# Linear attention on Trainium2: the turned query tile's affine steps and the key sums move from ScalarE to VectorE

## What is computed

```python
    qh = _split_heads(_layernorm(q @ wq, ln_gamma, ln_beta))
    kh = _split_heads(_layernorm(k @ wk, ln_gamma, ln_beta))
    vh = _split_heads(_layernorm(v @ wv, ln_gamma, ln_beta))
    q_prime = jax.nn.relu(qh) + EPS_K
    k_prime = (jax.nn.relu(kh) + EPS_K) * em
    vh = vh * em
    kv = jnp.einsum('bhnd,bhne->bhde', k_prime, vh)
    z = 1.0 / (jnp.einsum('bhnd,bhd->bhn', q_prime, k_prime.sum(axis=-2)) + EPS_K)
    att = jnp.einsum('bhnd,bhde,bhn->bhne', q_prime, kv, z)
```

## Time and profile before

| | us |
|---|---|
| median of three runs | 740.03 |
| the three runs | 743.93, 737.79, 740.03 |
| the profiled execution | 745.89 |
| its span in the profile | 744.1 |
| first stage in it | from the start to about 165 |

### The profile page before, as it was taken

One profiled execution on the slowest core, in us unless ns is written; L12 is line 12 of the kernel. 1 busy time (PEld: TensorE's weight loads), 2 busy tenths in 40 slices (PEclk: granted clock), 3 DMA queues, 4 the chain that ended last, 5 costly groups with the idle time before them and its releaser, 6 DMA issues.

```text
span 744.1 us, 19421 instructions
## 1 busy us (share of the span) xinstructions
PE 666.2 (90%) x7317; PEld 467.4 (63%) x7317; DVE 522.7 (70%) x1228; ACT 519.2 (70%) x875; POOL 270.2 (36%) x324
## 2 busy tenths in 40 slices
PE   6888889885468999999999999999999987999997
PEld 5677778773225666666665566566666664577777
DVE  5898889978778779878878878878876751212112
ACT  6788889878326887887787787787888866634441
POOL 6788889882243214304322422432233100000000
PEclk9999999999589999999999999999999999799999
DMA  5122222525523476356547636645664480201110
GB/s 186 43 84 83 83 83 83 160 86 31 121 74 86 92 167 142 92 130 135 128 92 142 152 92 145 135 109 111 135 155 114 87 192 8 61 30 57 29 43 26
DMA packets 59523, 74.42 MB, mean 100 GB/s; under 512 B 35464, under 2 KB 40322, under 8 KB 59450
## 3 DMA queue, kind: packets, MB, share of 16 engines
q1 hardware_dynamic: 59450, 73.39, 41.8%
HBM read 32.35 MB, written 1.40 MB: 45 GB/s over the span
## 4 chain that ended last, share of the span: by engine, by line
PE 42%; issue 12%; DVE 10%; POOL 5%; ACT 2%; SPq 1%; DMA 1%; DVEq 0%; POOLq 0%; ACTq 0%
PE ps L832 7%; PE ps L844 7%; PE ps L771 7%; PE ps L683 6%; DVE mx L1694 6%; PE ps L758 5%; PE ps L669 3%; PE ps L675 3%; POOL Qb L1221 2%; POOL QD L1235 1%; ACT P L1096 1%; DVE kvall L1525 1%; POOL KP L1207 1%; PE ps L705 1%; SPq L450 1%
## 5 line engine op out<-in xcount | busy, mean ns | idle before, releaser
L1096 ACT ACTIVATE P<-ps,kbias,kscale 125x896 f32<-125x896 f32 x192 | 210.3, 1097 | 86.2 <-PE ps L758 83.4
L1694 DVE TENSOR_REDUCE mx<-ps 128x1 f32<-128x500 f32 x336 | 213.9, 671 | 46.4 <-PE ps L683 45.0
L683 PE MATMUL ps<-KP,Qb 128*128 128x500 bf16 x336 | 128.8, 385 | 15.1 <-DVE mx L1694 9.9
L1207 POOL TENSOR_TENSOR KP<-kvall,KP 128x1500 bf16<-128x1500 f32 x16 | 48.6, 3038 | 230.8 <-ACT KP L1039 230.8
L771 PE MATMUL ps<-P,Vp 125*32 125x112 f32 x3072 | 113.6, 265 | 2.7 <-ACT P L1096 1.4
L771 PEld LDWEIGHTS ps<-P,Vp 125*32 125x32 f32 x3072 | 67.4, 109 | 53.0 <-issue 37.8
L543 PE MATMUL ps<-wkv,cT 128*125 128x256 f32 x384 | 93.0, 386 | 4.9 <-ACT wkv L895 4.9
L543 PEld LDWEIGHTS ps<-wkv,cT 128*125 128x125 f32 x384 | 69.8, 191 | 13.7 <-ACT wkv L895 4.9
L1157 ACT ACTIVATE arena<-ps,b 128x448 f32<-128x448 f32 x64 | 40.4, 633 | 47.5 <-PE ps L832 41.6
L561 PE MATMUL ps<-arena 125*128 125x130 f32 x384 | 54.9, 285 | 17.5 <-DVE arena L1399 15.1
L758 PE MATMUL ps<-QS,KS 128*128 128x112 bf16 x768 | 68.7, 214 | 1.4 <-DVE QS L1700 1.4
(11 more groups left out here) (217 smaller groups left out, 1031.1 us busy)
## 6 DMA issues: line engine op xcount, KB each, us to landing
cT<-ctxT_dram SPq DMA_DIRECT2D x31, 750.0 KB, 4.1
KS<-KP SPq DMA_DIRECT2D x48, 375.0 KB, 7.3
arena<-KP SPq DMA_DIRECT2D x48, 375.0 KB, 7.2
QS<-QD SPq DMA_DIRECT2D x96, 28.0 KB, 5.5
wgu<-w_dram SPq DMA_DIRECT2D x8, 256.0 KB, 3.2
silu<-w_dram SPq DMA_DIRECT2D x8, 256.0 KB, 3.0
x<-xh_dram SPq DMA_DIRECT2D x1, 512.0 KB, 4.0
cT<-ctxT_dram SPq DMA_DIRECT2D x1, 500.0 KB, 5.3
```

The costliest lines, as they stand in the source:

```text
L683: ins = nc.tensor.matmul(ps[:, bank, 0:KCW], q[:, 128 * c:128 * c + 128], KP[par][0][:, KCW * k:KCW * k + KCW], start=True, stop=True)
L1096: nc.scalar.activation(P[t % 2][0:TK, :].rearrange("p (k n) -> p k n", k=2), src, ACT.Exp, scale=kscale[0:TK, bass.ds(n, 1)], bias=kbias[0 ...
L1207: nc.gpsimd.tensor_tensor(KP[par][2][:], krest, KP[par][1][:], ALU.subtract).then_inc(sem("kp3_ready"), 1)
L1694: ins = v.tensor_reduce(mx[:, c, k:k + 1], ps[:, bank, 0:KCW], AX.X, ALU.max)
```

## The change

The relu and affine step of the turned query tile and its added constant, two ScalarE instructions, become two VectorE instructions: scale and shift by the two columns of `affine`, from PSUM to the same place in PSUM, and then maximum with 0 and the added constant, from PSUM to SBUF. Between them VectorE waits for its own result. They stand in the step of group 1, behind the keys, for tiles 0 to 6; for the last tile they stand in the end stage between the last state but one and the last clamp. The copy of the key sums goes from ScalarE to VectorE too, ahead of the state it belongs to; the wait of VectorE for ScalarE's copy goes. TensorE waits for the finished query tile where it waited for the relu.

```diff
                     if par == 0:
-                        pe.wait_ge(sem("qT_relu"), b // 2)
+                        pe.wait_ge(sem("qT_ready"), b // 2)
...
-            def turned_query(i, bank):
-
-                nc.scalar.activation(qT[:, bass.ds(D * i, D)], ps[:, bank, 0:D], ACT.Relu, scale=affine[:, 0:1],
-                                     bias=affine[:, 1:2]).then_inc(sem("qT_relu"), 1)
-
-            def raised_query(i):
-
-                cols = bass.ds(D * i, D)
-                nc.scalar.activation(qT[:, cols], qT[:, cols], ACT.Identity, bias=eps_in[:]).then_inc(sem("qT_ready"), 1)
...
-            def key_sums(b, par):
-
-                act.wait_ge(sem("kv_done"), NG * (b + 1) + SLOTS)
-                nc.scalar.copy(ks2[:, par:par + 1], ps[:, 6 + par, D:D + 1]).then_inc(sem("ks2_ready"), 1)
...
+            def turned_query(i, bank):
+
+                dve.wait_ge(sem("qT_ps"), i + 1)
+                v.tensor_scalar(ps[:, bank, 0:D], ps[:, bank, 0:D], affine[:, 0:1], affine[:, 1:2], ALU.mult,
+                                ALU.add).then_inc(sem("qT_normed"), 1)
+                dve.wait_ge(sem("qT_normed"), i + 1)
+                v.tensor_scalar(qT[:, bass.ds(D * i, D)], ps[:, bank, 0:D], 0.0, EPS_IN, ALU.max,
+                                ALU.add).then_inc(sem("qT_ready"), 1)
...
             def state(b, par):
 
                 dve.wait_ge(sem("kv_done"), NG * (b + 1) + SLOTS)
-                dve.wait_ge(sem("ks2_ready"), b + 1)
                 kv = ps[:, 6 + par, :]
+                v.tensor_copy(ks2[:, par:par + 1], kv[:, D:D + 1]).then_inc(sem("ks2_ready"), 1)
...
+                        if k == 1 and not first:
+                            turned_query(i - 1, 6)
...
             state(B - 2, 0)
+            turned_query(NT - 1, 3)
             relu(last, SLOTS - 1)
```

More of the change, by code:

```diff
@@ L975, in pair @@
                             query_rows(k - 3, 7)
-                        if g == 0 and not first:
-                            key_sums(2 * i + par - 2, par)
                         if k >= 4 and not first:
                             beta_queries(2 * i + k - 6, k - 4, i - 1)
-                        if k == 2 and not first:
-                            act.wait_ge(sem("qT_ps"), i)
                         if not (first and k < 1):
@@ L985, in pair @@
                             turned_rows(k - 1, 8 - k)
-                        if k == 2 and not first:
-                            turned_query(i - 1, 6)
                         if k == 3:
                             act.wait_ge(sem("q_var"), i + 1)
-                            if not first:
-                                act.wait_ge(sem("qT_relu"), i)
                         if k == 5:
@@ L996, in pair @@
                             query_deviation(i)
-                            if not first:
-                                raised_query(i - 1)
                         if k == 5:
@@ L1002, in _ @@
             in_pairs(act, pair, B // 2)
-            key_sums(B - 2, 0)
             values(NG * B - 1, SLOTS - 1)
-            act.wait_ge(sem("qT_ps"), NT)
-            turned_query(NT - 1, 3)
-            act.wait_ge(sem("qT_relu"), NT)
-            raised_query(NT - 1)
             beta_queries(B - 2, 0, NT - 1)
-            key_sums(B - 1, 1)
             beta_queries(B - 1, 1, NT - 1)
```

## The result

The changed kernel takes 745.81 us (median of 22 executions, 743.10 to 747.43), the kernel before 741.01 us beside it (22 executions, 737.13 to 746.25). The ratio is 1.0062, 95% interval 1.0044 to 1.0079: some 0.6% slower, which counts as no change by the bound of the forecast. Later series, on other occasions, gave other ratios, and why, as far as the runs show it, is the main thing here.

A forecast was written before the change was run, and what follows sets the result against it. First stage bound by GpSimd's floor plus lost VectorE-GpSimd races: 745.89 - 4 x 0.98 = 742.0, plus 0.8 for copies, less 0.2 at the end, less 1.0 for chance wins: 741.6 us. Own range 739 to 744; wider range 735.5 to 748.6.

The forecast's parts named there:

- what bounds the stage: First stage: a pair of batches takes 19.19 or 17.24 us; in the short one GpSimd, busy 16.77, is the floor.
- The race: VectorE's clamp against GpSimd's beta add: a clamp over about 0.02 us later waits for all of it; 0.98 us per loss.
- what the removed constant brings: ScalarE, group 4: square 0.20 us earlier, clamp wins by 0.17 to 0.20; group 0 then won by about 0.07.
- group 2 is lost: Pairs 1 to 6: new VectorE work delays norms and clamp, which loses to GpSimd's add by 0.06 us in a short pair.
- 0.39 + 0.16 + 0.20 = 0.75: VectorE, group 1: first turned-query instruction, gap behind it, second instruction, in us; bounds 0.51 and 1.16.
- pairs of 18.3 us: First stage of the changed profile: pairs of about 18.3 us, against 17.2 if races are won throughout.
- The copies: Two 128x1 key-sum copies on VectorE: 0.07 us each, 0.14 a pair, 0.8 over six pairs with a stall.
- a race lost by so little is won sometimes, as one in six was at group 4: less 1.0: Group 2, pairs 1 to 6: an occasional win takes 1.0 us off the sum, 742.6 to 741.6.
- losses do not breed: After a loss GpSimd idles until VectorE's keys of group 2; its later adds move back more than the norms of group 4.
- pair 7 "won": Pair 7, outside the loop: no register instruction, so 0.13 us less new work and the race is won.
- the end of the stage: Last state update no longer waits for ScalarE's copy and starts about 0.2 us earlier; that gain is kept.
- a run with two: Timed runs read by long pairs at 1.95 us each: median 740.03 us has two, the profiled 745.89 us five.

The follow-up runs named there:

- the split: Changed kernel with its second new VectorE instruction behind the clamp of group 2: 737.95 us, ratio 0.9917 in series 1; 738.58 us, 1.0004 in series 3.
- the query alone: Changed kernel with ScalarE's copies of the key sums put back, so only the turned query moves to VectorE: 744.61 us, ratio 1.0021.
- the forced kernel before: Kernel before, with GpSimd's beta add also waiting for the clamp of the group before at steps 1 and 3: 740.03 us, ratio 1.0022.
- the key sums alone: Kernel before with only the copy of the key sums moved to VectorE, turned query left on ScalarE: 740.64 us, ratio 0.9964.
- the query behind the clamp: Changed kernel with both new turned-query instructions behind the clamp of group 2: 742.72 us, ratio 1.0049.
- Forced: Changed kernel, with GpSimd's beta add also waiting for the clamp of the group before at steps 1 and 3: 741.11 us, ratio 1.0038.
- constant later: Kernel before, all work left on ScalarE, the turned query's added constant placed behind the square of group 4: 739.31 us, ratio 1.0026.

## Why the prediction was right, and where it was off

The class came out as forecast (within 1%), and 745.81 lies in the range of 735.5 to 748.6. The point of 741.6 does not: it is 4.2 us low, and the forecast's own range, 739 to 744, misses the measured time. In the comparison of kernels it said 0.2% above the kernel before; it was 0.6% in the first series and 0.9% in the third.

**Right: what bounds the stage.** The race, its price (2.05 us for two losses in pair 7 and 1.07 for the one of group 2, against 0.98 each), the starts that decide it. Swapping one instruction of the changed kernel past one clamp moved every one of six races, and the pairs from 18.3 to 17.25 us.

**Right: what the removed constant brings.** Groups 4 and 0 are won in all pairs of the loop but the one at 33.07, which the forecast left lost. The forecast said a win at group 4 by 0.17 to 0.20; it is 0.08 to 0.10, 0.1 less. Counted from the keys of group 3, the clamp comes 2.03 us later where it was 2.20, which is nearly the forecast's 0.20 earlier; but the add comes 2.12 later where it was 2.17, earlier too and not 0.03 later. The kernel with the constant moved shows the same cause with nothing else changed.

**Right: group 2 is lost.** The new work was put at 0.39 + 0.16 + 0.20 = 0.75; the trace has 0.41, a gap of 0.16 and 0.21 (from 75.07 to 75.28), 0.78 in all. By the Trainium skill's price from PSUM to SBUF (VectorE: DVE Perf Modes, section on the TRN2 errata: 120 cycles and one per element at 0.96 GHz) the first instruction would last an estimate of 0.26 us and the races be won. The page's row is for PSUM to SBUF, and for that form, the second instruction, the trace is near it: 0.28 to 0.29. The first writes PSUM, which the row does not cover, and took 0.41. The forecast's 0.39 was near because it added a price for two pointer scalars; whether the pointers or the write to PSUM cost the 0.12 to 0.13 above the second one, no run shows.

**Right in sum, with two parts off: pairs of 18.3 us.** A loss at group 2 costs 1.07 and not 0.98 (18.32 against the split's 17.25). The copies were put at 0.14 a pair, 0.8 in all, once a pair has a stall; the kernel with the query alone, which lacks them, has the same pairs (18.31 to 18.36) and the same length (144.55, against 144.59 in the changed kernel's second profile, both with 7 losses). So they cost nothing that shows. The two errors nearly cancel.

**Wrong: "a race lost by so little is won sometimes, as one in six was at group 4: less 1.0".** The margin here was 0.05 in pair 1 and 0.08 to 0.10 in the others, where 0.06 was reckoned, and no clamp 0.04 to 0.10 behind was won in any profile (the table below). None of twelve was won in two profiles of the changed kernel, nor of six with the query alone. The one in six of the kernel before came from margins of 0.00 to 0.04, at and around the point where it is open: it lost five, one and none of its six loop pairs in three profiles of one program.

**Wrong: "losses do not breed", and pair 7 "won".** Pair 7 has no register instruction; the gap behind L1342 is 0.03 there and its margin 0.02 to 0.03, in the middle of the undecided zone. Lost in one profile and won in the other, and won with the query alone. When lost, group 4 lost as well, by 0.07. That is 2.05 us in the profile and chance in the median.

**About right: the end of the stage, though the first look says otherwise.** The last state update was to start 0.2 earlier. It starts 2.57 us behind the last clamp where it was 3.89, 1.3 less. It waits for TensorE's matmuls now, no more for ScalarE:

```profile
167.18 0.16 DVE L1382 COPY ks<-ps 128x1 f32<-128x1 f32 x1 [0.86 <-PE ps L561]
167.26 0.28 DVE L1383 TENSOR_TENSOR kvall<-ps,gmask 128x128 f32<-128x128 f32 x1
```

But most of the 1.3 is the clock's. Ahead of the last state TensorE multiplies out the numerators (L579, L581). In the kernel before it did so at a granted clock of 0.62 (163.90 to 167.50), in the changed one at 1.00 (163.90 to 166.00). The split, one program, shows both, first in series 1 (clock 0.63 from 154.30 to 157.90), then in series 3 (1.00 from 154.30 to 156.70):

```profile
154.79 0.76 PE L579 MATMUL ps<-kvall,qT 128*64 128x144 f32 x4
```

```profile
154.63 0.47 PE L579 MATMUL ps<-kvall,qT 128*64 128x144 f32 x4
```

Its last state update starts 3.59 and 2.09 us behind its last clamp. With fast numerators the forced kernel before, whose copies are ScalarE's, has 2.26, and the key sums alone, the changed kernel's second profile and the split have 2.08 or 2.09: the 0.2 of the forecast. (The 2.57 belongs to the profile in which pair 7 lost two races.) With slow ones the kernel before has 3.88 or 3.89 in two profiles, the query alone 3.76 and the split 3.59. To the first exponential hardly any of it arrives: from the last clamp it is 60.32 to 60.65 in the changed kernel and the split, 60.44 to 62.07 in the kernel before.

**The sum again, from the profiled execution.** Forecast -4.3, measured +0.5, so 4.8 missed. The length was to fall by 4.1 (-3.9 + 0.8 - 1.0) and fell by 1.2: the chance win that did not come (1.0) and the two losses of pair 7 (2.05) make 3.05. The dearer loss and the copies that cost nothing leave 0.1 the other way. Outside the length the forecast had -0.2 and the profile has +1.7: the start by 0.8, the window stage and the tail by 1.0, at a clock of 0.960 instead of 0.970, less 0.14. These last are not of the change, since kernels without it have a rest of up to 599.2 too.

**What the forecast had in hand and did not carry through.** It read the timed runs by the number of long pairs, and named the median as a run with two. It summed from a profile with five. In its three profiles the kernel before lost between none and five of six pairs, and its median moved between 738.0 and 743.9 us from series to series (that the second follows from the first in every series is read from one profile in each of two, and argued for the rest), whereas the changed kernel lost six of six in both profiles, by a margin outside that zone (0.05 to 0.10), at 744.2 and 745.8. So the change trades a race that is often won for one that is always lost. Done from the median run instead, the sum has two long pairs to win back, 2 x 1.95, the one long clamp that pair 1 keeps either way, and pays 6 x 0.98 + 0.8: +2.8, or 742.8, on a median of 740.03, a ratio of 1.004. For the third series, in which the profiled kernel before had no long pair, the same sum gives 738.0 + 6.7 = 744.7; 744.2 were measured. The 0.8 in it stands for the dearer loss, not for the copies.

**Left open.** Why the kernel before lost many races in one series and few in another: a few hundredths of a microsecond between two engines decide, and no view of the profile shows what shifts them. The mean granted clock of the kernel before isn't it: 0.963, 0.964 and 0.965 in the three series. That the race is, as argued above, has one more sign: in the first series the kernel before ranged over 14 us in 29 executions, and the split, in whose profiles no clamp starts up to 0.04 behind an add, over 2.9 us in 8. And the 5 us of spread that remain with all pairs alike: in which stage they arise only one pair of profiles was read for (below), and no run tried to move them.

## What to carry to other kernels

Before a change to VectorE or GpSimd work in a loop where both read SBUF, list for each step the start of VectorE's instruction against GpSimd's. A step in which it stands from level to 0.04 us behind is a coin: the kernel's median can depend on the occasion, and a profile is only one throw of it. New VectorE work ahead of the instruction that races can lose the race, and behind it, it can hold up the engine that is the floor; cut in two, it cost nothing here, where the same work in one piece cost 1.07 us a pair ahead of the clamp and 0.58 behind it. Compare a change with the kernel's fastest pairs, and ask of each race not only whether it is won but by how much.

## What the runs showed of the hardware

**The race has an undecided zone of some hundredths of a microsecond.** All starts of a clamp and an add that lie within 0.12 us of each other, in the eleven profiles without a forced order:

| clamp starts | won (under 0.7 us) | lost (over 1.1 us) |
|---|---|---|
| up to 0.11 ahead, or together | 96 | 0 |
| 0.01 or 0.02 behind | 18 | 1 |
| 0.03 behind | 1 | 3 |
| 0.04 to 0.10 behind | 0 | 23 |

Whoever loses pays in its own duration (here the clamp 1.45 to 1.52 instead of 0.42, or the add up to 1.57 instead of 1.26), not in idle time, so no view of waits shows it. The Trainium skill has the exclusion as a rule (SBUF — State Buffer, section Who interferes with whom), and these counts agree with it, up to the 0.03. The new instructions with a PSUM source take no part, as that rule has it: L1342 lasts 0.41 at 74.50, beside a GpSimd add that ran from 73.50 to 74.84, and L1345 lasts 0.29 at 75.07, beside the multiply from 74.97 to 76.24. They last the same where GpSimd is idle: 0.42 at 159.87 in the kernel with the query behind the clamp, of which GpSimd works through 0.07, and 0.29 at 164.49 in the changed kernel.

**A wait for order didn't cure the exclusion.** Forced, the clamp of group 2 was always first, and the one of group 3 waited 0.5 us for the multiply that the wait had pushed back.

**A part of this kernel's spread goes with the TensorE clock, not with its code.** In the forced kernel before, whose pairs are all alike in its profile, the times ran from 737.0 at a mean granted clock of 0.969 to 742.2 at 0.960. A straight line through its ten times falls by 0.4 us for each 0.001 of clock, an estimate of 3.6 of the 5.2 us. Two kernels in the second series, constant later (clock 0.969) and query behind the clamp (0.958), in the same two windows behind the first stage (us; busy of PE, PEld, DVE, ACT, POOL; clock, DMA share, GB/s), first the one, then the other:

```profile
165.00:245.00 80.00, 53.45 (x475) 30.13 (x478) 64.64 (x176) 42.27 (x59) 23.48 (x36) 0.81 0.48 90
245.00:735.00 490.00, 462.96 (x5963) 314.09 (x5973) 311.81 (x749) 339.26 (x451) 106.56 (x132) 0.99 0.46 103
```

```profile
165.00:245.00 80.00, 55.63 (x433) 31.21 (x435) 63.42 (x179) 41.66 (x55) 23.47 (x36) 0.72 0.46 83
245.00:735.00 490.00, 466.49 (x6020) 316.46 (x6030) 314.27 (x750) 343.34 (x457) 106.56 (x132) 0.99 0.46 104
```

The clock differs where TensorE is less busy, between 165 and 245 us: 0.81 and 0.72, a mixture of its two levels of 1.2 and 2.4 GHz. The moment at which it fell there moved from one profile to the next, from about 165 to 185 us. In some profiles it was low for two or three microseconds in the numerators as well, in others not (above). But less than half of the difference between these two executions arises there. From the last clamp to the first exponential of the window stage they take 60.43 and 61.32 us, 0.9 apart; from there to the end 518.3 and 519.8, 1.5 apart, at clocks that both round to 0.99 from 245 us on. How much of the 5 us comes from the clock was not tried, and a correlation doesn't show which way the cause runs. Nor is it as close everywhere: -0.88 over the twelve times of the split in series 3, but -0.06 over its eight in series 1.
